# Cross-attention and mixture-of-experts kernel: the first shared-expert chunk moved ahead of the last batch's softmax, and TensorE a chunk ahead in the tail of the attention part

## The reference

```python
def _L0_xattn_ref(q, latent_kv, Wq, Wkv_expand, Wout):   # B 32, S 512->112, 16 heads of 32, latent 128
    qp = q @ Wq.T
    kv = latent_kv @ Wkv_expand.T
    ...
    scores = jnp.einsum('bhqd,bhkd->bhqk', qh, kh) * inv_sqrt_d
    scores = jnp.where(causal, scores, jnp.finfo(scores.dtype).min)
    attn = jax.nn.softmax(scores, axis=-1)
    ...
    return out @ Wout.T

def _L0_ffn_ref(x, gate_w, expert_fc1, expert_fc2, expert_proj, shared_fc1, shared_fc2, shared_proj, shared_gate_w):
    probs = jax.nn.softmax(xf @ gate_w.T)          # 8 experts, the 2 best weigh in
    h = jax.nn.silu(h1) * h2                       # per expert, 352 wide
    y = jnp.einsum('ne,enc->nc', combine, out_e)
    shared = jax.nn.silu(s1) * s2 @ shared_proj.T  # shared expert, 1408 wide
    y = y + jax.nn.sigmoid(xf @ shared_gate_w.T) * shared

x = x + _L0_xattn_ref(_layernorm(x), ctx_512, ...)
x = x + _L0_ffn_ref(_layernorm(x), ...)
```

## Time and profile before

| | |
|---|---|
| three runs | 1508.57, 1514.23, 1515.4 us; median 1514.23 |
| the profiled execution: own time | 1513.03 us |
| its span | 1511.3 us |
| mean granted PE clock | 0.99 of full |
| busy, of the span | PE 98%, DVE 59%, ACT 43%, POOL 41% |
| stretches | attention to about 430 us, tail 430 to 530, experts to 950, shared expert's other six groups to the end |

### The profile page before, as it was taken

One profiled execution on the slowest core, in us unless ns is written; L12 is line 12 of the kernel. 1 busy time (PEld: TensorE's weight loads), 2 busy tenths in 40 slices (PEclk: granted clock), 3 DMA queues, 4 the chain that ended last, 5 costly groups with the idle time before them and its releaser, 6 DMA issues.

```text
span 1511.3 us, 28047 instructions
## 1 busy us (share of the span) xinstructions
PE 1477.5 (98%) x9928; PEld 1256.4 (83%) x9928; DVE 894.0 (59%) x1453; ACT 653.0 (43%) x1833; POOL 617.5 (41%) x513
## 2 busy tenths in 40 slices
PE   7999999999789999999999999999999999999999
PEld 7888888887568899999999999887888888888887
DVE  6778888887555587876877867455223232233322
ACT  6999999998653323323323323332112121111211
POOL 3344566666343387685865864102101102011010
PEclk9999999999799999999999999999999999999999
DMA  6243445443155588867877765462303022030210
GB/s 232 80 118 117 124 114 133 125 120 93 52 132 117 155 324 323 270 254 262 284 249 267 267 221 179 167 216 86 97 15 112 28 69 63 8 111 28 64 48 28
DMA packets 102903, 217.42 MB, mean 144 GB/s; under 512 B 43696, under 2 KB 48816, under 8 KB 98064
## 3 DMA queue, kind: packets, MB, share of 16 engines
q1 hardware_dynamic: 91184, 184.71, 37.5%
q0 software_dynamic: 11616, 31.35, 7.1%
HBM read 168.86 MB, written 47.17 MB: 143 GB/s over the span
## 4 chain that ended last, share of the span: by engine, by line
PE 91%; ACT 4%; DVE 2%; DMA 1%; issue 1%; POOL 1%; POOLq 0%; SPq 0%; DVEq 0%; ACTq 0%
PE psum L827 64%; PE psum L1145 11%; PE psum L960 4%; ACT probs L1258 3%; PE psum L951 2%; PE psum L910 2%; PE psum L1047 2%; PE psum L982 2%; PE psum L1071 1%; PE psum L1012 1%; PE psum L969 1%; PE psum L941 1%; ACT probsT L1239 0%; DMA wkv_raw<-in_wkv 0%; POOL xn L1475 0%
## 5 line engine op out<-in xcount | busy, mean ns | idle before, releaser
L1582 POOL DMA_INDIRECT routed<-expert_out_dram,slot_b x56 | 56.8, 1014 | 478.0 <-DVE slot_b L2043 327.5
L2061 DVE TENSOR_TENSOR h_s<-psum,silu_s 128x512 f32<-128x512 f32 x66 | 45.6, 691 | 298.5 <-PE psum L827 298.5
L1258 ACT ACTIVATE probs<-psum,minus_max,rs 112x112 f32<-112x112 f32 x512 | 220.5, 482 | 2.2 <-DVE minus_max L1713 2.0
L827 PE MATMUL psum<-nT_hi,ws_hi 128*128 128x512 f32 x528 | 208.8, 395 | 3.1 <-DVE nT_lo L1984 2.8
L827 PE MATMUL psum<-nT_lo,ws_hi 128*128 128x512 f32 x528 | 208.6, 395 | 0.0
L827 PE MATMUL psum<-nT_hi,ws_lo 128*128 128x512 f32 x528 | 208.6, 395 | 0.0
L1554 POOL DMA_INDIRECT xg<-normed_dram,tile_ids x63 | 150.4, 2388 | 35.7 <-DMA tile_ids<-lists_dram 12.8
L827 PE MATMUL psum<-wj_hi,gT_hi 128*128 128x352 f32 x504 | 162.8, 323 | 0.0
L827 PE MATMUL psum<-wj_hi,gT_lo 128*128 128x352 f32 x504 | 162.3, 322 | 0.0
L827 PE MATMUL psum<-wj_lo,gT_hi 128*128 128x352 f32 x504 | 161.8, 321 | 0.0
L1372 ACT ACTIVATE silu_s<-psum 128x512 f32<-128x512 f32 x66 | 39.5, 598 | 241.3 <-PE psum L827 241.3
(11 more groups left out here) (252 smaller groups left out, 3534.2 us busy)
## 6 DMA issues: line engine op xcount, KB each, us to landing
wj_raw<-in_w_experts SPq DMA_DIRECT2D x35, 1408.0 KB, 6.6
wj_raw<-in_w_experts SPq DMA_DIRECT2D x35, 768.0 KB, 5.9
wj_raw<-in_w_shared SPq DMA_DIRECT2D x22, 768.0 KB, 5.8
expert_out_dram<-y_c SPq DMA_DIRECT2D x63, 256.0 KB, 3.2
base<-x_dram SPq DMA_DIRECT2D x8, 1024.0 KB, 5.8
xT_raw<-in_xT SPq DMA_DIRECT2D x32, 224.0 KB, 4.7
x_in<-in_x SPq DMA_DIRECT2D x32, 224.0 KB, 4.3
x_res<-in_x SPq DMA_DIRECT2D x32, 224.0 KB, 3.0
```

The costliest lines, as they stand in the source:

```text
L827: mm = pe.matmul(out_ap, u, v, start=(n == 0), stop=(n == last))
L1258: done = act.activation(probs[:, j % 2, 4 * r + m, :], psum[0:SEQ, r, m * SEQ:(m + 1) * SEQ], ACT.Exp, bias=minus_max[:, r, m:m + 1], scal ...
L1582: pool.indirect_dma_start(out=routed[:, b % 2, c, :], out_offset=None, in_=expert_out_dram, in_offset=bass.IndirectOffsetOnAxis(ap=slot_b[ ...
L2061: dve.tensor_tensor(h_s[:, :], bank(b), silu_s[:, :], ALU.mult).then_inc(emptied_b[b], 1)
```

## The change

Five edits. (1) In `TURNS`, `normT` takes bank 7 and `outT` bank 5 (they had 5 and 7), in all steps; `probsT` and `outT` of the tail's first step, (8,0), leave the table: they go to banks 0 to 3 and 0 and have two semaphores of their own, `last_filled` and `last_emptied`. (2) PE: `hidden0(0)` comes at the end of step (7,3), and in the tail each step does `proj`, ranks where due, `hidden0(c + 1)`, `normT`, router, `project0(c)`. (3) DVE: `chunk0(c)` comes before the copies and statistics of the step, `logits_out` behind the choices; the placing of slots at (8,3) and (9,3) thus comes after `chunk0`. (4) POOL: the normalised rows of a step come before `sum_chosen`. (5) SP: the chunk's weights are loaded before the step's stores.

```diff
@@ TURNS
-    TURNS += [((_j, "probsT", k), 1, (7, 5, 4, 6)[k]) for k in range(4)]
-    TURNS += [((_j, "normT", 0), "norm", 5), ((_j, "outT", 0), 1, 7),
+    TURNS += [((_j, "probsT", k), "out", (7, 5, 4, 6)[k]) for k in range(4)]
+    TURNS += [((_j, "normT", 0), "norm", 7), ((_j, "outT", 0), "out", 5),
@@ Turns.there
+        if lag == "out":
+            return self.there(g, j, 1) and g < self.batches // TB
@@
+        LAST_BANK, LAST_TURN = {"probsT": (0, 1, 2, 3), "outT": (0,)}, {"probsT": (1, 2, 3, 4), "outT": (5,)}
...
         def wait_emptied(eng, g, j, stage, part=0):
 
+            if in_last(g, stage):
+                eng.wait_ge(S["last_emptied"], LAST_TURN[stage][part])
+                return
@@ SP, body
+                    if g >= NG:
+                        tail_loads(g, j)
                     if j == 1 and before(g, NG - 1):
...
-                    if isinstance(g, int) and g >= NG:
-                        tail_loads(g, j)
@@ PE, hidden0 and project0
                 if c == 0:
                     pe.wait_ge(S["n0_split"], KC)
-                    wait_emptied(pe, NG, 0, "probsT", 1)
-                    wait_emptied(pe, NG, 0, "outT")
+                    wait_emptied(pe, NG - 1, TB - 1, "normT")
+                    wait_emptied(pe, NG - 1, TB - 1, "outT")
...
                 if c == 0:
-                    pe.wait_ge(S["exp_done"], 2 * NB)
+                    for i in range(KC):
+                        wait_emptied(pe, NG, 0, "probsT", i)
+                    wait_emptied(pe, NG, 0, "outT")
@@ PE, step
                 proj()
-                if is_late(g, 0):
-                    normT()
                 if is_late(g, -1) and j == 2:
                     ranks(g, j)
...
                 if is_late(g, 0):
-                    hidden0(first_chunk(g, j))
+                    hidden0(first_chunk(g, j) + 1)
+                    normT()
...
                 next_front(g, j)
+                if g == NG - 1 and j == TB - 1:
+                    hidden0(0)
@@ PE, body and tail
-                    if is_late(g, 0) and first_chunk(g, j):
-                        project0(first_chunk(g, j) - 1)
+                    if is_late(g, 0):
+                        project0(first_chunk(g, j))
...
             for c in TAIL_CHUNKS:
-                hidden0(c)
...
-                project0(c - 1)
+                if c + 1 < SC:
+                    hidden0(c + 1)
+                    project0(c)
@@ POOL, body
+                    if there(g, j, 3) and t - 3 >= FROM:
+                        rows(t - 3)
                     if j == 2 and routes(g):
                         sum_chosen(g - 1)
-                    if there(g, j, 3) and t - 3 >= FROM:
-                        rows(t - 3)
@@ DVE, front of a step, behind aT_lo
+                if is_late(g, 0):
+                    if g == NG + 1 and j == 2:
+                        logits_out(g, j)
+                        table_first()
+                    if first_chunk(g, j) == 0:
+                        pj0_low(0)
+                    chunk0(first_chunk(g, j))
@@ DVE, end of that front
                 if is_late(g, 0):
                     choices(g, j)
+                    if not (g == NG + 1 and j == 2):
+                        logits_out(g, j)
+                    if g == NG and j == 2:
+                        route_z(g)
@@ DVE, body (the same calls of logits_out, table_first and route_z are gone from chunk0)
-                    if isinstance(g, int) and g >= NG:
-                        if g == NG and j == 0:
-                            pj0_low(0)
-                        chunk0(first_chunk(g, j), g, j)
-                        if g == NG + 1 and j == 3:
-                            table_second()
+                    if g == NG + 1 and j == 3:
+                        table_second()
```

More of the change, by code:

```diff
@@ L485, in build_program, with in_last, bank_of, filled_of @@
         SPLITS.append((2, *WEIGHTS[2][1:]))
+        LAST_BANK, LAST_TURN = {"probsT": (0, 1, 2, 3), "outT": (0,)}, {"probsT": (1, 2, 3, 4), "outT": (5,)}
+        def in_last(g, stage):
+            return g == NG and stage in LAST_BANK
+        def bank_of(g, stage, part=0):
+            return LAST_BANK[stage][part] if in_last(g, stage) else turns.bank(stage, part)
+        def filled_of(g, stage, part=0):
+            return S["last_filled"] if in_last(g, stage) else filled[turns.bank(stage, part)]
+        def emptied_of(g, stage, part=0):
+            return S["last_emptied"] if in_last(g, stage) else emptied[turns.bank(stage, part)]
         def wait_filled(eng, g, j, stage, part=0):
+            if in_last(g, stage):
+                eng.wait_ge(S["last_filled"], LAST_TURN[stage][part])
+                return
             eng.wait_ge(filled[turns.bank(stage, part)], nth(g, j, stage, part))
         def wait_emptied(eng, g, j, stage, part=0):
+            if in_last(g, stage):
+                eng.wait_ge(S["last_emptied"], LAST_TURN[stage][part])
+                return
             eng.wait_ge(emptied[turns.bank(stage, part)], nth(g, j, stage, part))
@@ L957, in step @@
                     for i in range(4):
-                        b = take(g, j, "probsT", i)
+                        b = bank_of(g, "probsT", i) if in_last(g, "probsT") else take(g, j, "probsT", i)
                         for r in range(4):
@@ L961, in step @@
                                               probs[:, (j + 1) % 2, 4 * r + i, :], ident[0:SEQ, 0:SEQ])
-                        mm.then_inc(filled[b], 1)
+                        mm.then_inc(filled_of(g, "probsT", i), 1)
                 def normT():
@@ L976, in step @@
                     wait_emptied(pe, g, j - 1, "value")
-                    b = take(g, j, "outT")
+                    b = bank_of(g, "outT") if in_last(g, "outT") else take(g, j, "outT")
                     for m in range(KC):
@@ L983, in step @@
                                            probsT[:, h, :], start=True, stop=True)
-                    mm.then_inc(filled[b], 1)
+                    mm.then_inc(filled_of(g, "outT"), 1)
                 def proj():
@@ L1225, in attnT_high @@
                             wait_filled(act, g, j - 1, "proj")
-                        b = turns.bank("outT")
+                        b = bank_of(g, "outT")
                         wait_filled(act, g, j, "outT")
@@ L1236, in body @@
                         for i in range(4):
-                            b = turns.bank("probsT", i)
+                            b = bank_of(g, "probsT", i)
                             wait_filled(act, g, j, "probsT", i)
-                            act.activation(probsT[:, 4 * i:4 * i + 4, :].rearrange("s h q -> s (h q)"), bank(b, SEQ, GT), ACT.Copy).then_inc(emptied[b], 1)
+                            act.activation(probsT[:, 4 * i:4 * i + 4, :].rearrange("s h q -> s (h q)"), bank(b, SEQ, GT), ACT.Copy).then_inc(emptied_of(g, "probsT", i), 1)
                         if not there(g, j, 0):
@@ L1735, in step @@
                     dve.tensor_tensor(aT_lo[:, (j + 1) % 2, :, :].rearrange("p k s -> p (k s)"), bank(b, P, GT),
-                                      hi.bitcast(F32), ALU.subtract).then_inc(emptied[b], 1)
+                                      hi.bitcast(F32), ALU.subtract).then_inc(emptied_of(g, "outT"), 1)
+                if is_late(g, 0):
[5 more added lines that the diff above has]
+                    chunk0(first_chunk(g, j))
                 if there(g, j, 2):
@@ L1907, in pj0_low, with chunk0 @@
                                   ALU.subtract).then_inc(S["pj0_split"], 1)
[L1909 to L1912, removed]
+            def chunk0(c):
                 if c + 1 < SC:
@@ L1923, in chunk0 @@
                 dve.tensor_tensor(h_0[:, :], bank(7), silu_0[:, :], ALU.mult).then_inc(h2_emptied, 1)
-                if g == NG and j == 2:
-                    route_z(g)
                 dve.wait_ge(S["hs0_hi_made"], c + 1)
```

4 lines of the change are left out of this document (1 added, 3 removed).

## The result

The changed kernel takes 1523.48 us (median of 5, 1522.18 to 1525.11) against 1510.79 for the kernel before (5 runs beside it, 1508.57 to 1515.4): **ratio 1.0075, 95% interval 1.0058 to 1.0093**, slower. 1521.5 was forecast. The profiled execution took 1524.11, its span is 1522.4.

What follows compares the result with a forecast made beforehand. PE was taken as the bound, the chain for 91% of the span. Earlier gains were used up before the last rank; tokens 3.7 later plus 4.5 of clock gave 8.2, so 1521.5 us, range 1514 to 1527.

Steps and rivals of the forecast that it cites:

- Part 1: Step (7,2): with POOL's `rows` ahead of `chosen`, PE's wait for `xn` goes; a gain of 9.3 us.
- Part 2: Pause behind router (7,3): hidden0(0) fills PE's 4.75 us idle; net shift there 8.7, plus 0.9 of half clock.
- Part 3: PE up to the last rank: new waits 1.4, 2.4, 0.5, 3.5 and 2.8 of extra work; rank at 487.6.
- Part 4: Last rank to tokens: stalls of 5.8 at hidden0(7) and 6.5 before the tokens; tokens 3.7 us later.
- Part 5: PE's clock: half-speed stretches behind the three new stalls cost 0.9, 1.7 and 1.9, together 4.5 us.
- The clock stays: Rival: quickest gathers, or stalls cost no clock; 1516 us, or 1518.5 at half the clock's price; chance 0.38.
- ACT and DVE keep up: Tail rival: early silu(3) and covered copies, 1513 us; second half, `fc_lo`(7) before `table_first` too, 1506; chances 0.05 each.
- The bank swap costs: Steady loop rival: `aT_lo` comes 0.3 late in each of 28 steps, 8 us more, 1529; chance 0.04.

Runs made afterwards that it cites:

- e5: The kernel before with only POOL's order changed: normalised rows ahead of `sum_chosen`; 1503.35 us, ratio 0.9942 to the kernel before.
- e6: The changed kernel with POOL's order as before, `sum_chosen` ahead of the normalised rows; 1532.9 us, ratio 1.0126 to the kernel before.
- e1: The changed kernel with the last group's slots placed on DVE before chunk 7, at (9,3); 1511.59 us, ratio 0.9998 to the kernel before.
- e4: The changed kernel with SP loading the first expert's weights behind the first three lists of ids; 1523.44 us, ratio 1.0071 to the kernel before.
- e2: The changed kernel with DVE's chunk 6 work ahead of the last ranks' copy, gate and table at (9,2); 1513.8 us, ratio 1.0014.
- e9: e7 with chunk 3's silu ahead of the router's exponentials at (8,3) and the last slots ahead of the table; 1503.33 us, ratio 0.9917.
- e3: The changed kernel with both DVE edits, those of e1 and e2; 1504.84 us, ratio 0.9949 to the kernel before.
- e11: e9 with chunk 0's silu ahead of the four evacuations of (8,0) on ACT; 1498.81 us, ratio 0.9895 to the kernel before.
- e12: The kernel before with only the banks of `normT` and `outT` swapped; 1512.4 us, ratio 0.9988 to the kernel before.
- e7: e3 with `normT` ahead of `hidden0` in tail steps and `proj` at (8,0) waiting for `outT` of (7,3) alone; 1504.3 us, ratio 0.9944.

## Why the prediction was right, step by step

**Part 1 (9.3) right.** Scores (7,2) to (7,3) took 13.32 against a forecast 13.2. Added alone (e5) POOL's order is worth 8.5, and taken away (e6) 8 to 9.4.

**Part 2 (8.7) right.** From scores (7,2) to L985 of (8,0) it is 28.0 instead of 37.0: 9.0.

**Part 3 right but for one term.** `aT_lo` 1.38 (1.4 forecast), `xn2T` three times 0.91 (2.4 forecast, 2.7 measured), the silu of chunk 0 0.29 (0.5). The mis-sized term is the stall at hidden0(4): 3.5 forecast, 2.13 in e1, where PE stayed at full clock, 0.71 in the changed kernel, where most of project0(2) ran at half clock and filled the rest. The step that failed is "from the first load to the silu's end 5.0". ACT of the changed kernel at (8,3), against the earlier trace rows:

```profile
447.83 1.28 ACT L1298 ACT_TABLE_LOAD   x1
455.55 0.23 ACT L1298 ACTIVATE rt_e<-rt_z 112x32 f32<-112x32 f32 x1 [6.43 <-DVE rt_g L1820]
...
457.36 1.28 ACT L1240 ACT_TABLE_LOAD   x1
458.66 0.60 ACT L1240 ACTIVATE silu<-psum 128x512 f32<-128x512 f32 x1
```

The first load ran 7.7 ahead of its exponentials, in ACT's idle time, and its 1.28 left the path; only the second counts. The silu again starts 1.30 behind the start of its load, and the load directly behind the operation before it. The Trainium skill puts a switch at about 2.66 us ("ScalarE: Activation LUTs", What ACT_TABLE_LOAD costs), which would have made this stall 2.8 longer; these rows do not bear it out.

The last rank, forecast for 487.6, stood at 484.27; with scores (7,2) 2.1 earlier in this execution that is 486.4 on the scale of before. The forecast was 1.2 too late, about what this term was too large (3.5 against 2.13).

**Part 4: both stalls right, the second too small.** hidden0(7) waited 5.58 for `fc_lo` (5.8 forecast). The stall at the tokens was 10.77 against 6.5. From the rank to the tokens 53.65 passed instead of 45.9, and the last scatter came 27.9 behind the rank instead of about 25. Of the 7.8 more, hidden0(7) at half clock is 3.2 (1.7 of it stood in part 5); gather behind scatter is 2.6 and its landing 2.8, and the path from `h` to the last scatter gave 0.8 back. The step that failed is "to the gather 13.8 more, and its landing takes 6.6": I took both as constants of the chain, and for the landing the median, though the earlier trace rows have 9.3 as the longest. In the changed kernel SP issued 1408 KB of weights 0.4 before the last scatter, in the kernel before 4.3 behind it. e4 shows that this is the cause for the ids. For the longer landing of the gather the cause is open. POOL's row of this gather lasts 3.08 instead of 0.99, which is 2.1 of the 2.8; it lasts 3.10 in e2 and e6, the two other kernels with the weights just ahead of the last scatter, and 1.00 or less in all others, e4 among them. No run separates the weights from what else comes with them.

**Part 5 (4.5) right as a sum, by luck.** Forecast were 0.9, 1.7 and 1.9; measured are nothing behind the first stall, 3.2 in hidden0(7) and 1.4 behind the tokens: 4.6. The two levels of the clock are those of the windows above: both long stalls were followed by a stretch at 0.50. The Trainium skill says that activity releases the throttle ("TensorE: Matmul & The Clock Gate", What's actually happening), and these two stretches agree. A stall is not the whole story: in (8,3) the clock of the changed kernel fell to half as well, at 455.5, and since hidden0(1) PE had waited no longer than 0.91 at a time:

```profile
456.00:458.00 2.00, 2.00 (x6) 1.59 (x5) 1.15 (x2) 1.98 (x3) 0.00 (x0) 0.50 0.20 46
```

e1 has the same wait and stayed at full clock there; what made the difference is open.

**The rivals.** "The clock stays" fell (windows); it had held that a stall of 3.5 may cost no clock, and e9's 3.37 did cost it. "ACT and DVE keep up" fell for the changed kernel. e3, which mends DVE's order alone, takes 1504.8, near the 1506 of its second half, but without the silu and the copies that this rival also asks for; e9 and e11, which have them, take 1503.3 and 1498.8. "The bank swap costs" fell by e12. Against the runs beside it the loss is 0.75%, 11.3 us, or 12.7 by the medians, and 8.2 was forecast: the late lists and gather, and the half clock's full length in hidden0(7), are the difference. That 1521.5 lies within 2 of 1523.48 is partly luck: it was added to a median of 1514.23 of three runs, and the five runs beside the change have 1510.79.

Behind the tokens little more is lost: from the first to the last tokens 404.7 before, 406.1 after; the 1.4 are the half clock. From the last tokens to the end it is 576.7 to 579.8 in the profiles, 576.8 and 578.4 for the two kernels and 578.5 for e12, without order; I leave these 1 to 3 us as the spread of single executions.

## What to carry to other kernels

Putting one engine a step ahead moves the deadline of everything it reads. List, for each of its new positions, who makes the operand, and what stands in front of that on the maker's engine: here DVE had 7.7 us of idle time just ahead of the place where it became 5.6 late, and moving a call mended it. A small step at the head of a long chain of DMAs is worth the front place on its engine: here six instructions that place slots are 1.3 us of work and were worth 10 us of time. And take the parts of a combined change apart: 8.5 us of gain were one swapped pair of calls, and the rest cost twice that. Only with seven more edits, one wait after the other, did the rest earn its 5 to 7 us.

## What the runs showed that I had not expected

- With a load of 1408 KB issued 0.4 us ahead of the last small indirect scatter, the slowest of them landed in 12.7 us (8.3 before), and the ids that wait for all of them came 13.5 behind it (8.6 before). With the load behind the ids (e4) it was 6.6 and 7.5.
- An activation table load at the head of a group that waits can be off the path: in the changed kernel at (8,3) it ran 7.7 us before its first user.
- A half clock stretch can be free: in (8,3) it lay in products that a wait would have followed anyway (0.71 of wait at half clock, 2.13 at full in e1), and it came with no long idle before it.
- Taking away waits of 4.1 us shortened the sum of intervals by 1.3 (e7), two more edits by 1.0 (e9), and the last one by 3.5 (e11; 0.22% by the ratios): what a wait is worth shows only once the next one behind it is gone.
